# Self attention of a PixArt block: y is turned one step later, and VectorE takes its work of a step in another order

## The chip, the cores and the metric

One core of one Trainium2 chip runs the whole program. The metric is the device time of one execution, in microseconds, as the median of several runs; lower is better. The profile is of one execution, taken by the hardware profiler, and its times count from the start of its span.

## The reference

A transformer block on x of 16 batches, 224 tokens and 512 channels, with a context of 750 tokens: self attention with 16 heads of 32 channels, modulated by a condition, then cross attention on the context, then an MLP. The part that this change touches is the self attention and the query projection of the cross attention:

```python
x_norm = modulate(_ln(x), shift_a, scale_a)
qkv = x_norm @ W_qkv + b_qkv
attn_w = softmax(einsum('bhqd,bhkd->bhqk', q, k) * scale)
attn_out = einsum('bhqk,bhkd->bhqd', attn_w, v) @ W_proj + b_proj
x = x + gate_a[:, None] * attn_out
q_c = _ln(x) @ W_qc + b_qc
```

## The kernel before

The program has three phases one after another: self attention, cross attention, MLP. Each projection is made of three products of a split into a high and a low part (helper `product`, lines 71 to 73), so it takes three matmuls for each piece of 128 input channels.

The self phase is a pipeline over batches that is written out by hand. One body per batch has 16 steps, one per head; 19 bodies run, the last three to drain what lags. In step h of body b each engine runs its own list for that step, and every engine is a queue in order:

- TensorE (`pe`): the transposed scores of a head that lags by six (`score_t`, L487), the first projection of the step, the turning of row maxima at the end of a group of four heads (`turn_maxima`, L473), the scores of head h+1 (`score`, L455), the second projection of the step, if any, the value product and the sums of a group (`pv` L504 and `sums` L511, in steps 2, 6, 10, 14), and the turnings of x or y (`turn_x`, `turn_y`, both through `trans`, L418).
- VectorE (`dve`): the copy of turned maxima (`copy_maxima`, L714), normalisation of a group (`normalize`, L719 reciprocal and L722 product, in steps 0, 4, 8, 12), the row maxima of head h+1 (`row_max`, L701), their split into two parts in every fourth step (`split_maxima`, L707, L709), the evictions of the step's projections (`evict`: `lows` L656 for k, q and c, `add_bias` L666 for p, nothing for v), then the modulation of turned x (`modulate`, L649), the low part of turned y (`low_y`, L675), and others.
- ScalarE: the exponentials (L907), the high part of an eviction (L893, ahead of VectorE's `lows`), the high part of turned y (L918), the high part of o (L913), the layer norms (L875).
- GpSimd: the sum of two halves of the exponentials (L1017), the residual (L1025, L1027), the low part of x (L1009).

`FILL` is the table that says which projections and turnings are in which step: `("k", c, part)` is half `part` of the projection k of bank c. Letters k, q, v work for the next batch, p for the previous one, c (the query of the cross attention) for that two or three back. `tx` turns x of the batch two ahead (steps 12 and 13), `ty` turns y of the batch two back. An eviction follows the second half of a projection (`part == 1`). There is one bank of PSUM for each c, so the next projection on a bank waits until the last one is evicted (`bank_free`). `turn_x` for c == 1 waits for the modulation of c == 0 (`xT_v`), since both use the bank `tx_ps`; `turn_y` for c == 1 waits for `low_y` of c == 0 (`yT_l`) for the same reason, and for c == 0 it waits for the copy of the group's maxima (`m_row`), which use that bank too. Scores have two banks: `score` of a head waits for the row maxima of the head two before. `pv` of a group waits for `normalize` of the group before it (`o_done`).

Body 0 has no projections p and c, body 1 none of c, and body 1 has two products of the modulation (L561) in steps 13 and 14. From body 14 on no x is turned, and in body 15 there are no projections k, q, v.

Of the kernel before, what the change touches and what calls it, by code (L numbers as in the profile page):

```python
# [62 lines left out]
def wait(eng, sem, value):  # L63

    if not (isinstance(value, int) and value <= 0):
        eng.wait_ge(sem, value)
# [38 lines left out]
def self_phase(nc, x, cond_t, w_mod, b_mod, w_qkv, b_qkv_t, w_proj, b_proj, w_qc, b_qc_t, gates, x1, qc, mod_t,  # L105
# [3 lines left out]
    with ExitStack() as ctx:  # L109
# [109 lines left out]

        FILL = [[("c", 1, 1), ("k", 0, 0)], [("k", 0, 1)], [("k", 1, 0)], [("k", 1, 1), ("ty", 0, 0)],
# [3 lines left out]
        BANKS = [f for step in FILL for f in step if f[0][0] != "t" and f[2] == 0]  # L226

        def of(f):

            return -3 if f == ("c", 1, 1) else {"k": 1, "q": 1, "v": 1, "p": -1, "c": -2, "tx": 2, "ty": -2}[f[0]]  # L230

        def exists(b, f):
            return 0 <= b.c + of(f) < B and b.c >= -1

        def fills(b, h, kinds):
            return [(*f, b.plus(of(f))) for f in FILL[h] if f[0] in kinds and exists(b, f)]

# [23 lines left out]
        def far(b):  # L261
            return b.c < B - 2
# [11 lines left out]
        def late_group(b, h, att, prv):  # L274

            if h % HPG != (LAG + HPG) % HPG:
                return []
            g = (h - LAG - HPG) // HPG
            if g >= 0:
                return [(b, g)] if att else []  # L280
            return [(b.plus(-1), g + KC)] if prv else []
# [344 lines left out]
        def _(dve):  # L626
# [26 lines left out]
            def lows(b, c, high, low, bias, first_chunk, dst):  # L653
                dve.wait_ge(high, b.n(2, c + 1))
                for m in range(2):
                    last = dve.scalar_tensor_tensor(out=dst[1][:, 2 * c + m], in0=pj_ps[c][:, m * N:(m + 1) * N],  # L656
                                                    scalar=bias[:, first_chunk + m:first_chunk + m + 1],
                                                    in1=dst[0][:, 2 * c + m].bitcast(F32), op0=ALU.add, op1=ALU.subtract)
                last.then_inc(low, 1)

            def add_bias(b, t):
                dve.wait_ge(proj_ps, b.n(2, t + 1))
                wait(dve, x1_out, b.n(32, 0))
                if b.c == 0:
                    dve.wait_ge(bproj_in, 16)
                dve.tensor_tensor(y[:, t], pj_ps[t][0:QN, :], bproj[:], ALU.add).then_inc(proj_done, 1)  # L666
# [16 lines left out]
            def stats_context(t):  # L683
                dve.wait_ge(c_loaded[t], 16)
                dve.bn_stats(st_c[:, t], c_in[:, t]).then_inc(stats_c, 1)
# [12 lines left out]
            def row_max(b, h):  # L698
                g, j = h // HPG, h % HPG
                dve.wait_ge(scored, b.n(NH, h + 1))  # L700
                dve.tensor_reduce(nmax[:, g % 2, :, j], sc_ps[h % 2][0:QN, 0:QT * N].rearrange("p (t k) -> p t k", t=QT), AX_X, ALU.max,  # L701
                                  negate=True).then_inc(maxed, 1)

            def split_maxima(b, g):
                dve.wait_ge(maxed, b.n(NH, HPG * (g + 1)))
                wait(dve, m_ps, b.n(KC, g - 1))
                dve.tensor_copy(nsplit[:, g % 2, :, 0], nmax[:, g % 2]).then_inc(m_h, 1)  # L707
                dve.wait_ge(m_h, b.n(KC, g + 1))
                dve.tensor_tensor(nsplit[:, g % 2, :, 1], nmax[:, g % 2], nsplit[:, g % 2, :, 0].bitcast(F32), ALU.subtract).then_inc(m_l, 1)  # L709

            def copy_maxima(b, g):
                dve.wait_ge(m_ps, b.n(KC, g + 1))
                wait(dve, m_in, b.n(16 * KC, 16 * g))
                dve.tensor_copy(mrow[:], tx_ps[0:2 * HPG, 0:N]).then_inc(m_row, 1)  # L714

            def normalize(b, g):
                dve.wait_ge(sum_ps, b.n(KC, g + 1))
                wait(dve, o_done, b.n(KC, g))
                dve.reciprocal(rb[:], or_ps[:, R0:R0 + N]).then_inc(inverted, 1)  # L719
                dve.wait_ge(pv_done, b.n(KC, g + 1))  # L720
                dve.wait_ge(inverted, b.n(KC, g + 1))
                dve.tensor_tensor(ou[:], or_ps[:, 0:N], rb[:], ALU.mult).then_inc(o_done, 1)  # L722

            def evict(kind, c, part, o):
                if kind == "k" and part == 1:
                    lows(o, c, k_h, k_l, bqkv, KC + 2 * c, nat)
                if kind == "q" and part == 1:
                    lows(o, c, q_h, q_l, bqs, 2 * c, natq)
                if kind == "c" and part == 1:
                    lows(o, c, c_h, c_l, bqcs, 2 * c, natq)  # L730
                if kind == "p" and part == 1:
                    add_bias(o, c)

            def body(b, att, nxt, prv, old):
                z, y2, far_b = b.plus(-1), b.plus(-2), b.plus(2)
                for h in range(NH):
                    if h % HPG == HPG - 1 and att:
                        copy_maxima(b, h // HPG)
                    for o, g in late_group(b, h - 2, att, prv):
                        normalize(o, g)  # L740
                    if h < NH - 1 and att:
                        row_max(b, h + 1)
                    if h == NH - 1 and nxt:
                        row_max(b.plus(1), 0)
                    if h % HPG == HPG - 2 and att:
                        split_maxima(b, h // HPG)
                    for f in fills(b, h, "kqcp"):
                        evict(*f)
                    for _, c, _, o in fills(b, h, ("tx",)):
                        modulate(o, c)  # L750
                    for _, c, _, o in fills(b, h, ("ty",)):
                        low_y(o, c)
                    if h == 14 and att:
                        low_o(b, 0)
                    if h in LOW_O and prv:
                        low_o(z, LOW_O[h])
                    if far(b) and h == 6:
                        stats(far_b, x_in, x_loaded, lambda t: far_b.n(16, 0), st1, mv1, stats1, mvs1)
                    if far(b) and h == 8:
                        neg_mean(far_b, mv1, rs1, nm1, rstd1, nmr1)  # L760
                    if prv and h == 15:
                        stats(z, y, summed, lambda t: z.n(2, t + 1), st2, mv2, stats2, mvs2)
                    if old and h == 0:
                        neg_mean(y2, mv2, rs2, nm2, rstd2, nmr2)
                    if b.c == 0 and 2 <= h < 2 + KC:
                        low_w(3 * KC + h - 2)
                    if b.c == 1 and h == 0:
                        gate_rows(3)
                    if b.c == 1 and h in (13, 14):
                        mlp_row(h - 9)  # L770
                    if b.c == 1 and h == 15:
                        keep_modulation()
                    if b.c == 2 and 5 <= h < 5 + KC:
                        low_w(4 * KC + h - 5)
                    if b.c == B - 1 and 5 <= h < 5 + KC:
                        low_wkv(h - 5)
                    if b.c == B - 1 and 9 <= h < 9 + ST:
                        stats_context(h - 9)
                    if b.c == B and h == 0:
                        aggregate_context()  # L780
                    if b.c == B and h == 2:
                        neg_mean_context()
# [302 lines left out]
def cross_phase(nc, ctx_in_dram, b_kvc_t, qc, o_dram, wkv, c_in, cT, nat, pieces, ident, neg_half, eps):  # L1085
# [4 lines left out]
    with ExitStack() as ctx:  # L1090
# [50 lines left out]

        FILL = [[("k", 0, 0)], [("k", 0, 1)], [("k", 1, 0)], [("k", 1, 1)], [], [("k", 2, 0)], [("k", 2, 1)], [], [("v", 0)], [("k", 3, 0)], [("k", 3, 1), ("c", 0)], [("v", 1), ("c", 1)], [("v", 2), ("c", 2)], [("v", 3), ("c", 3)], [("v", 4), ("c", 4)], [("v", 5), ("c", 5)]]
        ORDER = [f for step in FILL for f in step if f[0] != "c"]

# [23 lines left out]
        def fill_at(b, h, kinds):  # L1168

            return [(f, b) for f in FILL[h] if f[0] in kinds and exists(b, f[0])]  # L1170

# [29 lines left out]

        STEP = {f[1]: h for h, step in enumerate(FILL) for f in step if f[0] == "c"}

# [998 lines left out]
```

## Time and profile before

| what | value |
|---|---|
| median of 3 runs | 2776.03 us (2774.58 to 2776.41) |
| span of the profiled execution | 2771.8 us |
| TensorE busy | 2667.6 us (96%) |
| VectorE busy | 1743.5 us (63%) |
| GpSimd busy | 1296.9 us (47%) |
| ScalarE busy | 1118.3 us (40%) |
| self phase | from 0 to about 770 us |
| one body of it in the steady part | 43.4 us |

A busy TensorE is not one at its peak: its matmuls are pipelined and their ends are modelled, so the distance from one start to the next says more than the busy time. An idle time in brackets at the end of a row, with the releaser, counts from the modelled end of the instruction before; the real loss is found from starts.

### The profile page before, as it was taken

To read this page: it belongs to the slowest core of one execution; us is meant where nothing else is said; L and a number is where in the kernel's file an instruction comes from. 1 tells how busy PE (TensorE), PEld (TensorE's weight loads), DVE (VectorE), ACT (ScalarE), POOL (GpSimd) and SP (SyncE) were. 2 spreads that over 40 slices of the span, in tenths; PEclk is the share of its full clock that TensorE was granted. 3 is DMA by queue.
4 is the path that set the end of the run, shared out by engine and by line. 5 is a ranking of instruction groups with operands and counts; after the bars stand their busy time and mean duration, and the time that the engine had idled before them with its cause. 6 is when DMAs were issued, how large, how long until landed. Compare 5 with 4: busy or idle time off the path is not lost. (4 is left out here: it accounts for less than half of the span.)

```text
span 2771.8 us, 50094 instructions
## 1 busy us (share of the span) xinstructions
PE 2667.6 (96%) x18676; PEld 2153.0 (78%) x18676; DVE 1743.5 (63%) x3285; ACT 1118.3 (40%) x2187; POOL 1296.9 (47%) x1447
## 2 busy tenths in 40 slices
PE   8999999999789999999999999999889999999997
PEld 6788888887677778777877877777568888888886
DVE  6777777777636777777777766776754444444431
ACT  4344444444434555555545555554532212112110
POOL 2344545444414676776676676666811220220211
PEclk9999999999899999999999999999789999999999
DMA  8454453545252443444344434433431111111110
GB/s 225 125 129 122 124 138 106 130 121 144 91 136 77 110 110 105 106 109 115 105 108 117 108 103 117 109 80 96 126 110 39 36 52 35 42 46 35 42 42 23
DMA packets 169359, 269.86 MB, mean 97 GB/s; under 512 B 28928, under 2 KB 83200, under 8 KB 169104
## 3 DMA queue, kind: packets, MB, share of 16 engines
q1 hardware_dynamic: 166048, 259.33, 34.5%
q0 software_dynamic: 3072, 7.34, 0.8%
q8 instruction: 150, 2.46, 0.4%
q14 instruction: 89, 0.73, 0.1%
HBM read 111.11 MB, written 36.77 MB: 53 GB/s over the span
## 5 line engine op out<-in xcount | busy, mean ns | idle before, releaser
L1490 DVE TENSOR_REDUCE cross_nmax<-cross_sc_ps 112x1 f32<-112x750 f32 x512 | 459.6, 928 | 162.7 <-PE cross_sc_ps L1365 162.6
L1608 ACT ACTIVATE cross_prT<-cross_tr_ps 125x448 f32<-125x448 f32 x768 | 389.9, 544 | 153.5 <-PE cross_tr_ps L1384 146.2
L1655 POOL TENSOR_TENSOR cross_part<-cross_prT 125x448 f32<-125x448 f32 x252 | 290.9, 1154 | 149.4 <-PE cross_or_ps L1404 83.4
L1017 POOL TENSOR_TENSOR self_psum<-self_prT 112x224 f32<-112x224 f32 x256 | 173.3, 677 | 349.4 <-ACT self_prT L907 337.0
L1384 PE MATMUL cross_tr_ps<-cross_qst,cross_kst 98*125 98x224 f32 x1536 | 314.4, 291 | 8.5 <-ACT cross_prT L1608 3.9
L1384 PEld LDWEIGHTS cross_tr_ps<-cross_qst,cross_kst 98*125 98x125 f32 x1536 | 244.6, 190 | 92.8 <-ACT cross_prT L1608 39.2
L1657 POOL TENSOR_TENSOR cross_part<-cross_part,cross_prT 125x448 f32<-125x448 f32 x252 | 291.9, 1158 | 19.8
L2052 ACT ACTIVATE mlp_hv<-mlp_h_ps,mlp_b 128x512 f32<-128x512 f32 x112 | 77.1, 689 | 519.8 <-PE mlp_h_ps L73 505.7
L1365 PE MATMUL cross_sc_ps<-cross_kst,cross_qst 96*112 96x500 f32 (+1 forms) x1024 | 274.2, 350 | 5.5 <-DVE cross_nmax L1490 2.3
L1969 DVE CAST mlp_hT_h<-mlp_hv 128x512 fp32r<-128x512 f32 x112 | 53.5, 477 | 319.1 <-ACT mlp_hv L2052 319.1
L907 ACT ACTIVATE self_prT<-self_st_ps 112x448 f32<-112x448 f32 x256 | 139.1, 544 | 210.6 <-PE self_st_ps L487 210.5
L701 DVE TENSOR_REDUCE self_nmax<-self_sc_ps 112x2 f32<-112x448 f32 x256 | 157.7, 617 | 79.5 <-PE self_sc_ps L455 78.5
L1659 POOL TENSOR_TENSOR cross_psum<-cross_part 125x224 f32<-125x224 f32 x252 | 170.2, 675 | 19.8
L71 PE MATMUL mlp_a_ps<-mlp_w_l,mlp_hT_h 128*128 128x512 f32 x448 | 178.3, 398 | 0.0
L72 PE MATMUL mlp_h_ps<-mlp_xT_h,mlp_w_l 128*128 128x512 f32 x448 | 177.5, 396 | 0.0
L72 PE MATMUL mlp_a_ps<-mlp_w_h,mlp_hT_l 128*128 128x512 f32 x448 | 176.9, 395 | 0.0
L73 PE MATMUL mlp_h_ps<-mlp_xT_h,mlp_w_h 128*128 128x512 f32 x448 | 176.7, 395 | 0.0
L73 PE MATMUL mlp_a_ps<-mlp_w_h,mlp_hT_h 128*128 128x512 f32 x448 | 176.6, 394 | 0.0
L71 PE MATMUL mlp_h_ps<-mlp_xT_l,mlp_w_h 128*128 128x512 f32 x448 | 176.6, 394 | 0.0
L71 PE MATMUL cross_pj_ps<-cross_cT_l,cross_wkv_h 128*128 128x374 f32 (+1 forms) x492 | 168.3, 342 | 4.3 <-DVE cross_nat_l L1484 4.3
L73 PE MATMUL cross_pj_ps<-cross_cT_h,cross_wkv_h 128*128 128x374 f32 (+1 forms) x492 | 165.5, 336 | 0.0
L1397 PE MATMUL cross_or_ps<-cross_prT,cross_vt 125*32 125x224 f32 x3072 | 164.8, 364 | 0.6 <-ACT cross_prT L1608 0.6
(247 smaller groups left out, 6644.9 us busy)
## 6 DMA issues: line engine op xcount, KB each, us to landing
cross_kst<-cross_nat_h SPq DMA_DIRECT2D x512, 93.8 KB, 2.2
cross_c_in<-in_context SPq DMA_DIRECT2D x96, 250.0 KB
cross_kst<-cross_nat_l SPq DMA_DIRECT2D x256, 93.8 KB, 2.2
cross_qst<-qc SPq DMA_DIRECT2D x192, 112.0 KB, 2.4
self_kst<-self_nat_h SPq DMA_DIRECT2D x128, 112.0 KB, 2.3
self_qst<-self_natq_h SPq DMA_DIRECT2D x128, 112.0 KB, 3.1
self_x_in<-in_x SPq DMA_DIRECT2D x16, 448.0 KB, 3.8
self_kst<-self_nat_l SPq DMA_DIRECT2D x64, 112.0 KB, 2.3
```

The source lines that it names most:

```text
L71: pe.matmul(out, lhs[0], rhs[1], start=first, stop=False)
L72: pe.matmul(out, lhs[1], rhs[0], start=False, stop=False)
L73: return pe.matmul(out, lhs[0], rhs[0], start=False, stop=last)
L1017: pool.tensor_tensor(psum[:, j], prT[:, j, 0], prT[:, j, 1], ALU.add).then_inc(p_summed, 1)
L1365: last = pe.matmul(sc_ps[t][0:QN, SC0 + c0:SC0 + c0 + cn], qst[0:TERMS * HD, g, j, t * QN:(t + 1) * QN], kst[0:TERMS * HD, g, j, c0:c0 + c ...
L1384: last = pe.matmul(bank(step, c)[0:SN, m * N:(m + 1) * N], kst[:, g, j, kt * SN:(kt + 1) * SN], qst[:, g, j, :], start=True, stop=True)
L1397: last = pe.matmul(or_ps[HD * j:HD * j + HD, 0:N], vt[:, b.par, kt, h * HD:h * HD + HD], prT[:, slot(h), kt], start=kt == 0, stop=kt == ST ...
L1490: dve.tensor_reduce(nmax[:, g % 2, t, j:j + 1], sc_ps[t][0:QN, SC0:SC0 + S], AX_X, ALU.max, negate=True).then_inc(maxed, 1)
L1608: act.activation(prT[:, slot(h), 2 * c:2 * c + 2], bank((h + LAG) % NH, c)[0:SN, 0:2 * N].rearrange("p (k t) -> p k t", k=2), ACT.Exp).the ...
L1655: pool.tensor_tensor(part[:], prT[:, j, 0:2], prT[:, j, 2:4], ALU.add).then_inc(pre_summed, 1)
L1657: pool.tensor_tensor(part[:], part[:], prT[:, j, 4:6], ALU.add).then_inc(pre_summed, 1)
L1659: pool.tensor_tensor(psum[:, j], part[:, 0], part[:, 1], ALU.add).then_inc(p_summed, 1)
```

## The change

Two things. In the table `FILL` the two turnings of y move from steps 3 and 4 to steps 4 and 5; TensorE's `turn_y`, ScalarE's high part and VectorE's low part follow, since all three read the table. In VectorE's list of a step, the eviction that belongs to the step's first entry now stands right behind the copy of maxima, then come the row maxima and their split, then the evictions of the other entries, and then normalisation, which stood ahead of the row maxima. The letter v is added to the kinds only so that "first entry" counts it; its eviction does nothing on VectorE.

```diff
-        FILL = [[("c", 1, 1), ("k", 0, 0)], [("k", 0, 1)], [("k", 1, 0)], [("k", 1, 1), ("ty", 0, 0)],
-                [("q", 0, 0), ("ty", 1, 0)], [("q", 0, 1), ("q", 1, 0)], [("q", 1, 1)], [("v", 0, 0)],
+        FILL = [[("c", 1, 1), ("k", 0, 0)], [("k", 0, 1)], [("k", 1, 0)], [("k", 1, 1)],
+                [("q", 0, 0), ("ty", 0, 0)], [("q", 0, 1), ("q", 1, 0), ("ty", 1, 0)], [("q", 1, 1)], [("v", 0, 0)],
                 [("v", 0, 1), ("v", 1, 0)], [("v", 1, 1)], [("p", 0, 0)], [("p", 0, 1), ("p", 1, 0)],
                 [("p", 1, 1), ("tx", 0, 0)], [("c", 0, 0), ("tx", 1, 0)], [("c", 0, 1)], [("c", 1, 0)]]
...
                 for h in range(NH):
                     if h % HPG == HPG - 1 and att:
                         copy_maxima(b, h // HPG)
-                    for o, g in late_group(b, h - 2, att, prv):
-                        normalize(o, g)
+                    for f in fills(b, h, "kqcpv")[0:1]:
+                        evict(*f)
                     if h < NH - 1 and att:
                         row_max(b, h + 1)
                     if h == NH - 1 and nxt:
                         row_max(b.plus(1), 0)
                     if h % HPG == HPG - 2 and att:
                         split_maxima(b, h // HPG)
-                    for f in fills(b, h, "kqcp"):
+                    for f in fills(b, h, "kqcpv")[1:]:
                         evict(*f)
+                    for o, g in late_group(b, h - 2, att, prv):
+                        normalize(o, g)
```

## Rows read from the trace of the kernel before

**Rows 1.** The page's first part: busy time, share of the span, instructions.
```profile
PE 2667.6 (96%) x18676; PEld 2153.0 (78%) x18676; DVE 1743.5 (63%) x3285; ACT 1118.3 (40%) x2187; POOL 1296.9 (47%) x1447
```
**Rows 2.** Who TensorE waited for, 130 to 660: total us, times, longest us.
```profile
PE self_tx_ps L418 <- DVE self_mrow L714: 3.4, 13, 0.3
PE self_pj_ps L71 <- DVE self_natq_l L656: 2.7, 12, 0.2
```
**Rows 3.** Timeline, TensorE, steps 2 and 3 of body 6: start, length, [idle before].
```profile
300.87 0.38 PE L487 MATMUL self_st_ps<-self_qst,self_kst 98*112 98x224 f32 x2
301.46 0.37 PE L71 MATMUL self_pj_ps<-self_xT_l,self_wqkv_h 128*128 128x224 f32 x1 [0.22 <-DVE self_natq_l L656]
...
306.24 0.44 PE L455 MATMUL self_sc_ps<-self_kst,self_qst 96*112 96x224 f32 x2
306.94 0.60 PE L418 MATMUL self_tx_ps<-shared_ident,self_x_res 112*128 112x112 f32 x4 [0.26 <-DVE self_mrow L714]
```
**Rows 4.** Timeline, TensorE, where it waits for nothing: score, score_t, projection.
```profile
317.56 0.44 PE L455 MATMUL self_sc_ps<-self_kst,self_qst 96*112 96x224 f32 x2
317.84 0.37 PE L487 MATMUL self_st_ps<-self_qst,self_kst 98*112 98x224 f32 x2
318.05 0.39 PE L71 MATMUL self_pj_ps<-self_wqkv_l,self_xT_h 128*112 128x512 f32 x1
```
**Rows 5.** Timeline, VectorE, step 12 of body 6, whole.
```profile
329.54 1.53 DVE L719 RECIPROCAL self_rb<-self_or_ps 128x224 f32<-128x224 f32 x1
331.18 0.39 DVE L722 TENSOR_TENSOR self_ou<-self_or_ps,self_rb 128x224 f32<-128x224 f32 x1
331.51 0.63 DVE L701 TENSOR_REDUCE self_nmax<-self_sc_ps 112x2 f32<-112x448 f32 x1
332.05 0.68 DVE L666 TENSOR_TENSOR self_y<-self_pj_ps,self_bproj 112x512 f32<-112x512 f32 x1
332.65 0.92 DVE L649 TENSOR_SCALAR self_xv<-self_tx_ps,shared_mod_t 128x224 f32<-128x224 f32 x2
```
**Rows 6.** Timeline, TensorE, the end of step 12 and of step 13 of body 6.
```profile
330.87 0.39 PE L73 MATMUL self_pj_ps<-self_wproj_h,self_oT_h 128*112 128x512 f32 x1
...
333.63 0.60 PE L418 MATMUL self_tx_ps<-shared_ident,self_x_in 112*128 112x112 f32 x4
```
**Rows 7.** Timeline, TensorE, the second projection of step 0 of body 7.
```profile
341.00 0.28 PE L71 MATMUL self_pj_ps<-self_xT_l,self_wqkv_h 128*128 128x224 f32 x1
...
342.50 0.27 PE L487 MATMUL self_st_ps<-self_qst,self_kst 98*112 98x224 f32 x1
```
**Rows 8.** Windows: us, busy (instructions) of PE, PEld, DVE, ACT, POOL; PEclk, DMA, GB/s.
```profile
68.20:71.00 2.80, 0.00 (x0) 0.00 (x1) 2.70 (x6) 0.36 (x2) 1.11 (x2) 1.00 0.82 182
72.20:75.40 3.20, 3.20 (x29) 1.60 (x28) 2.68 (x5) 1.00 (x2) 1.81 (x2) 0.50 0.00 0
686.60:689.80 3.20, 1.45 (x12) 1.10 (x10) 3.05 (x8) 1.39 (x4) 1.67 (x4) 1.00 0.01 2
690.00:710.30 20.30, 18.10 (x100) 12.40 (x100) 17.25 (x31) 11.46 (x20) 7.52 (x9) 0.50 0.35 115
809.40:816.10 6.70, 5.17 (x28) 4.28 (x28) 1.95 (x3) 2.36 (x5) 0.00 (x0) 1.00 0.56 132
```
**Rows 9.** Timeline, TensorE, like matmuls at 1.2 GHz, then at 2.4 GHz.
```profile
758.37 0.41 PE L73 MATMUL self_pj_ps<-self_yT_h,self_wqc_h 128*128 128x224 f32 x1
758.58 0.41 PE L71 MATMUL self_pj_ps<-self_yT_l,self_wqc_h 128*128 128x224 f32 x1
...
762.38 0.27 PE L71 MATMUL self_pj_ps<-self_yT_l,self_wqc_h 128*128 128x224 f32 x1
762.49 0.28 PE L72 MATMUL self_pj_ps<-self_yT_h,self_wqc_l 128*128 128x224 f32 x1
```
**Rows 10.** Timeline, the split of maxima on VectorE and GpSimd's residual, step 14.
```profile
336.69 0.73 DVE L707 CAST self_nsplit<-self_nmax 112x8 fp32r<-112x8 f32 x1
...
336.11 1.28 POOL L1027 TENSOR_TENSOR self_y<-self_y,self_x_res 112x512 f32<-112x512 f32 x1
```

## The prediction

> **What bounds the kernel now.** The page's first part says that TensorE is busy for 96% of the span and VectorE for 63% [rows 1], so the program is as long as TensorE's work plus what TensorE loses in waits. The change touches the self phase alone, about 770 us, and there its steady part: bodies 2 to 14, 43.4 us each. Next I read who TensorE waited for in that part. The answer has two lines [rows 2]: 13 waits of the first turning of y (L418) for the copied maxima, and 12 of the projection in step 2 (L71) for an eviction of c. The reader should see that these are exactly the two things that the diff loosens, and that they are small. Then I read the timelines of TensorE and VectorE of body 6, since every body repeats them within some hundredths. The lost time is to be taken from starts, not from the idle time in brackets, because the ends are modelled.
>
> **Removed: the wait in step 2.** The eviction of c on bank 1 stands behind normalisation and a reduction in step 0 and ends late. The projection starts 0.59 us after the `score_t` ahead of it [rows 3]; where nothing is waited for, that distance is 0.21 us [rows 4]. So 0.38 us is lost, 12 times [rows 2]: 4.6 us. With the eviction first in step 0 it ends about 2 us earlier, and the wait is gone for good.
>
> **Removed: the wait of the first turning of y.** It starts 0.70 us after the score [rows 3]; a score behind a turning of maxima otherwise gives way after 0.28 us [rows 4]. So 0.42 us, 13 times: 5.5 us. One step later its maxima have been copied for some 2 us.
>
> **Moved: the second turning of y, to the end of step 5.** It waits for VectorE's low part of the first, which now stands behind normalisation in step 4. VectorE needs there 0.54 for a reduction, 1.97 for a normalisation (both below) and for the low part about what a reduction over as many columns takes, 0.63 [rows 5]: 3.1 us from the score of step 4. TensorE has meanwhile a turning, `score_t`, two projections of twelve matmuls at 0.11 us [rows 9] and a score, about 3.4 us. It fits with 0.1 to 0.3 us to spare, so I cost it at nothing; the other bound is 0.3 us in 13 bodies, 4 us. ScalarE's high part of o comes behind the high part of y in step 5, under a microsecond later, and nobody waits for it before step 10. On SyncE's queue the load of x for the residual follows the maxima of step 7, so it doesn't see the move.
>
> **Added: normalisation behind an eviction, in step 12.** This is the costly one. In step 12 VectorE now does, in a row [rows 5]: reciprocal 329.54, product 331.18, row maxima 331.51, `add_bias` 332.05, modulation of the first half of x 332.65 to 333.57. At 333.63 TensorE turns the second half of x [rows 6], which waits for just that modulation: the chain already touches TensorE. The reader should see that normalisation runs while TensorE is still at the projection p of that step, whose last matmul starts at 330.87 and ends at 331.26 [rows 6]: it costs nothing there. In the new order VectorE comes first to `add_bias`, which needs that projection. Normalisation waits behind it in the queue though everything that it needs is there. The new chain, in the clock of body 6: `add_bias` 331.30; its distance to the next instruction 0.60 (332.65 - 332.05), so row maxima at 331.90; 0.54 (332.05 - 331.51), so normalisation at 332.44; 1.64 to the product and 0.33 to the next (331.18 - 329.54, 331.51 - 331.18), so modulation at 334.41; 0.92 long, so 335.33; and 0.06 to TensorE's start as now (333.63 - 333.57): 335.39 instead of 333.63. I take 1.75 us per body; the bounds, from overlaps of up to a tenth at each end, are 1.6 and 1.9.
>
> It doesn't happen in every body. From body 14 on no x is turned. Body 0 has no projection p, so nothing stands ahead of normalisation. In body 1 TensorE has eight matmuls of the modulation between the two turnings, long enough to hide it. Bodies 2 to 13 are left: 12 times 1.75, 21.0 us.
>
> **Given back by the longer body.** The second projection of step 0 takes 1.50 us from its first start to the next instruction [rows 7], against 12 times 0.11, 1.32 [rows 9]: it waits for GpSimd's low part of x inside. GpSimd's work doesn't get later by the stall, so this 0.18 us goes, 12 times: 2.2 us.
>
> **The other steps with normalisation.** In steps 0, 4 and 8 it ends 1 to 1.6 us later against TensorE. Its readers on TensorE (`pv` two steps later) stand about 3 us behind, and ScalarE, which waits longer for it in step 8, is ahead of TensorE by more than a step. Cost nothing, bound 0.1 us per body.
>
> **Body 15 and the tail.** Body 15 has no second projection in step 0, so TensorE waits 2.1 us for row maxima there and is then granted half the clock for 20 us (0.50 from 690.0 to 710.3) [rows 8]. The new order gives the maxima 1 us earlier and normalisation 1.5 us later, for which `pv` waits: about +0.3. If the clock stayed up, VectorE, busy for 17.25 of these 20.30 us [rows 8], leaves at most 3 us to gain. So 0, bounds -3 and +2. The bodies behind it drain and hold nothing of the change that is longer than some tenths.
>
> **The sum without the clock.** -4.6 - 5.5 - 2.2 + 21.0 = +8.7 us. The profiled execution spans 2771.8 us, 4.2 us under the median; the sum stands for both: 2776.0 + 8.7 = 2784.7.
>
> **The clock.** The new idle time is 1.75 us more than the wait of some 0.2 us that is there now, so about 1.9 us in one piece, in each of 12 bodies. What idle time does to TensorE's clock here: after nothing ran from 68.20 to 71.00 the granted clock was 0.50 (1.2 GHz) from 72.20 to 75.40; after the 2.1 us idle in body 15 it was 0.50 for 20 us; around an idle time of 1.53 us (6.70 less 5.17, from 809.40 to 816.10) it stayed at 1.00 (2.4 GHz) [rows 8]. The new idle time lies between 1.5 and 2.1 us. I take it that half of the 12 bodies, six, see a drop. The short one here covers the whole of 72.20 to 75.40, so I take 3.4 us for one at the lower clock; there like matmuls start every 0.21 us instead of every 0.11 [rows 9]: 3.4 times (1 - 0.11/0.21) = 1.6 us. Six are 9.7 us; none and twelve are the bounds, 0 and 19. The long drop of body 15 isn't taken: TensorE was short of work there, while behind the turning of x a projection of twelve matmuls and a value product are ready.
>
> **A rule that bears on the split of maxima.** In steps 6 and 14 it now comes behind an eviction, about 0.4 us ahead of the turning that needs it. The row of step 14 shows a cast that took 0.73 us and ended at 337.42, as GpSimd's residual did at 337.39 [rows 10]. The Trainium skill, page SBUF — State Buffer, section "Who interferes with whom", says that VectorE, in a two-port mode or with two inputs in SBUF, and GpSimd take one shared pair of ports for a whole instruction, and that the later one blocks. By that rule the split, moved against GpSimd's work, could be held again; the trace agrees that it can. In rows: a GpSimd sum or product of 0.7 to 1.3 us hides 0.4 us of margin and would cost 0.3 to 0.6 us in some bodies. It is a rival below.
>
> **The rivals.** (a) The stall is there, but the clock holds: 2785. For it: 1.53 us didn't drop it. Against: 2.1 us did. (b) Not slower: step 12 costs TensorE nothing, because VectorE reaches modulation in time. It decides at 12.3 us of gain over 12 bodies, so at 1.0 us of new stall per body: `add_bias` through modulation would have to take 3.3 us rather than 4.1. Without a stall: 2776.0 - 12.3 = 2764. Against it stands the sum of five rows in one queue; for it, only that a projection's end is modelled. (c) More waits: the split held by GpSimd and the second turning of y late by its bound: 0.5 us in 12 bodies on top of the forecast, 2801. (d) The clock stays low for 20 us after each drop as in body 15: a drop then costs 20 times 0.48, 9.6 us, six of them 58: 2843.
>
> **How the numbers follow.** Forecast, stall and about six short drops: 0.50, 2784.7 + 9.7 = 2794, itself 2787 to 2806. (a) 0.27, 2781 to 2788. (b) 0.07. (c) 0.11, 2797 to 2810. (d) 0.05. The range from 2780 to 2806 leaves out (b), (d) and part of (c). A measurement of this kernel can tell about 0.2%, 5.5 us, from no change: faster is under 2770.5, slower over 2781.5. Faster 0.05 of (b); same 0.02 of (b) and 0.07 of the low end of (a), where fewer bodies stall; slower the rest, 0.86.
>
> **What would show it.** Right: TensorE waits for modulation (L649) about 1.9 us in 12 bodies, after which VectorE's order is `add_bias`, row maxima, reciprocal, product, modulation; both lines of [rows 2] are gone; the distance between bodies is about 44.2 us where the clock holds. Wrong: the second turning of x starts within 0.4 us of its score; or a wait at L473 for the split (L709), or of the second turning of y for L675. The granted clock behind each stall tells the forecast from (a) and (d). The figure most open is the number of drops.

## The result and the profile after

The changed kernel takes 2792.1 us (four runs, 2790.4 to 2795.3) against 2776.2 us before; the ratio is 1.0055, 95% interval 1.0043 to 1.0068. Forecast was 2794 in a range from 2780 to 2806, slower with 0.86. The profiled execution spans 2793.2 us, 21.4 us more than that of before; it is the slowest of the four runs.

Who TensorE waited for in bodies 2 to 14 of the changed kernel, from 130 to 680: total us, times, longest us.

```profile
PE self_tx_ps L418 <- DVE self_xv L649: 21.5, 12, 2.1
PE self_or_ps L504 <- ACT self_prT L909: 0.4, 1, 0.4
```

Both lines of [rows 2] are gone. In their place stands one that before had not: 12 waits of the second turning of x for the modulation, 21.5 us: 1.76 us in eleven of the bodies and 2.1 us in body 8. The timeline of VectorE in step 12 of one body, and of TensorE at the end of steps 12 and 13 of it:

```profile
339.67 0.69 DVE L666 TENSOR_TENSOR self_y<-self_pj_ps,self_bproj 112x512 f32<-112x512 f32 x1 [1.69 <-PE self_pj_ps L73]
340.28 0.62 DVE L701 TENSOR_REDUCE self_nmax<-self_sc_ps 112x2 f32<-112x448 f32 x1
340.81 1.55 DVE L719 RECIPROCAL self_rb<-self_or_ps 128x224 f32<-128x224 f32 x1
342.46 0.39 DVE L722 TENSOR_TENSOR self_ou<-self_or_ps,self_rb 128x224 f32<-128x224 f32 x1
342.77 0.92 DVE L649 TENSOR_SCALAR self_xv<-self_tx_ps,shared_mod_t 128x224 f32<-128x224 f32 x2
```

```profile
339.24 0.39 PE L73 MATMUL self_pj_ps<-self_wproj_h,self_oT_h 128*112 128x512 f32 x1
...
341.62 0.37 PE L455 MATMUL self_sc_ps<-self_kst,self_qst 96*112 96x224 f32 x2
343.75 0.61 PE L418 MATMUL self_tx_ps<-shared_ident,self_x_in 112*128 112x112 f32 x4 [1.76 <-DVE self_xv L649]
```

These are the instructions of [rows 5] and [rows 6] in their new order. VectorE is idle for 1.69 us ahead of `add_bias`, the time in which it had normalised before. From the end of the projection (339.63) to TensorE's start (343.75) the chain takes 4.12 us; the forecast had 4.13.

The granted clock, one row for each of bodies 2 to 13, from the first score of one to that of the next. The columns are those of [rows 8]; the number ahead of the last two is TensorE's clock.

```profile
124.87:171.45 46.58, 43.79 (x375) 36.66 (x373) 35.07 (x75) 22.02 (x45) 22.03 (x27) 0.96 0.46 118
171.45:215.45 44.00, 42.24 (x379) 36.25 (x377) 32.53 (x72) 20.41 (x42) 20.60 (x27) 1.00 0.46 122
215.45:261.07 45.62, 43.86 (x379) 37.87 (x377) 32.53 (x72) 20.49 (x42) 20.89 (x27) 0.96 0.45 118
261.07:305.07 44.00, 42.24 (x379) 36.26 (x377) 32.53 (x72) 20.41 (x42) 20.92 (x27) 1.00 0.46 122
...
393.07:440.43 47.36, 45.25 (x379) 38.43 (x377) 32.52 (x72) 20.48 (x42) 20.89 (x27) 0.93 0.44 114
440.43:486.04 45.61, 43.85 (x379) 37.80 (x377) 32.52 (x72) 20.48 (x42) 20.59 (x27) 0.96 0.45 117
...
618.05:663.66 45.61, 43.85 (x380) 37.86 (x377) 32.53 (x72) 20.48 (x42) 20.91 (x27) 0.96 0.46 118
sum 538.79, PE 516.31 PEld 442.39 DVE 392.88 ACT 246.82 POOL 251.33; mean PE 43.03 PEld 36.87 DVE 32.74 ACT 20.57 POOL 20.94
```

A body is 44.00 us long where the clock held (before: 43.38) and 45.61 us where it dropped once; body 2 is 1 us longer for other reasons, with and without a drop. Five of the twelve have a drop; that at 0.93, 47.36 us long, has one twice as long, and is the body with the wait of 2.1 us. The five rows left out at "..." are like the one of 44.00 us. VectorE is busy for 32.5 us in either kind of body: the 1.6 us are TensorE's alone.

Where the 21.4 us of the profiled execution lie, from the starts of bodies: 2.5 us up to body 2; 18.6 us in bodies 2 to 13 (538.79 against 520.20); -0.5 us in body 14; 3.2 us in the drain; and -2.2 us in the cross and MLP phases, where nothing was changed. Over all traces of this case these two phases take 1996.5 to 2000.2 us, so 3 us of a single execution can come from there alone; the comparisons of bodies below are free of it.

### The profile page after: what moved, and what is told of

Its sections match the earlier page's. It is cut to its first block and busy times, and to the rows that moved or that the text cites. A ratio compares the mean times of both kernels' runs of the same rounds, so it can differ in the third digit from the quotient of the medians.

```text
span 2793.2 us, 50094 instructions
## 1 busy us (share of the span) xinstructions
PE 2666.8 (95%) x18676; PEld 2158.8 (77%) x18676; DVE 1738.7 (62%) x3285; ACT 1115.7 (40%) x2187; POOL 1304.0 (47%) x1447
## 5 line engine op out<-in xcount | busy, mean ns | idle before, releaser
L1019 POOL TENSOR_TENSOR self_psum<-self_prT 112x224 f32<-112x224 f32 x256 | 184.9, 722 | 342.3 <-ACT self_prT L909 333.5
L72 PE MATMUL cross_pj_ps<-cross_cT_h,cross_wkv_l 128*128 128x374 f32 (+1 forms) x492 | 165.5, 336 | 0.0
```

The source lines that it names most:

```text
L72: pe.matmul(out, lhs[1], rhs[0], start=False, stop=False)
L1019: pool.tensor_tensor(psum[:, j], prT[:, j, 0], prT[:, j, 1], ALU.add).then_inc(p_summed, 1)
```

## The experiments

Two theories stand against each other at first. T: the loss is made in step 12 alone, where normalisation waits behind `add_bias`, and all else is gain. R: it is spread over the four normalisations of a body, and the late turning of y adds to it. A third question is what part of the loss is the clock (theory C).

**The table alone.** The edit is that of the change in `FILL`; VectorE's list is that of before.

> The kernel before with the table of the change alone (y turned in steps 4 and 5, VectorE's order as before). Two theories. T: the whole loss of the change is made in step 12, where normalisation stands behind add_bias, and the move of y is a gain. R: the loss is spread over the four normalisations of a body, a quarter each, and the late turning of y adds to it. T expects the wait for copied maxima at L418 to be gone in 13 bodies, bodies 0.4 to 0.5 us shorter (43.38 to about 42.9 us), so 13 times 0.48, -6 us: 2770, 2768 to 2773. R expects no gain or a loss: 2776 or more.

It takes 2768.9 us, ratio 0.9973 (0.9961 to 0.9984). What TensorE waited for in bodies 2 to 14:

```profile
PE self_pj_ps L71 <- DVE self_natq_l L656: 2.4, 12, 0.2
```

The wait for copied maxima is gone, that of step 2 is left, and a body is 42.89 us long, 0.49 us shorter. The late turning of y is a gain.

**VectorE's order alone.** Here `FILL` is that of before.

> VectorE's new order alone, y turned in steps 3 and 4 as before. T: all that the change lost and 6 us more, since the gain of the table is missing: 2792 + 6 = 2798 (2794 to 2803), with the stall of 1.76 us ahead of the second turning of x in bodies 2 to 13, and the wait for copied maxima back. R: less than the whole change, about 2786 to 2790, since the late turning of y is undone.

2797.4 us, ratio 1.0073 (1.0061 to 1.0086). Its waits in bodies 2 to 14:

```profile
PE self_tx_ps L418 <- DVE self_xv L649: 21.4, 12, 2.1
PE self_tx_ps L418 <- DVE self_mrow L714: 3.4, 13, 0.3
```

The new order carries the whole loss, and the table took some of it back: 5 us by the medians, 44.48 us for a body against 44.00.

**Step 12 in the old order, all else changed.**

```diff
+                    if h == 12:
+                        for o, g in late_group(b, h - 2, att, prv):
+                            normalize(o, g)
                     for f in fills(b, h, "kqcpv")[0:1]:
                         evict(*f)
...
-                    for o, g in late_group(b, h - 2, att, prv):
-                        normalize(o, g)
+                    if h != 12:
+                        for o, g in late_group(b, h - 2, att, prv):
+                            normalize(o, g)
```

> The changed kernel, with normalisation back at the head of step 12 and nowhere else. T: no stall ahead of the second turning of x and no drop of the granted clock in bodies 2 to 13; what is left are the gains, 6 us of the table and 5.6 us of step 2, less some 5 us that body 1 and the drain lose by the new order: 2770, 2766 to 2773. R: a quarter of the loss goes, so about 2785 to 2788.

2773.1 us, ratio 0.9989 (0.9980 to 0.9998): 19 us less than the changed kernel, by one normalisation of four put back. That is at the upper edge of what T expected, and R is out. But it is slower than the table alone, and the reason is a wait that was not there before (waits in bodies 2 to 14, then VectorE, GpSimd and TensorE in steps 14 and 15 of one body):

```profile
PE self_tx_ps L473 <- DVE self_nsplit L709: 5.9, 12, 0.5
```

```profile
338.11 0.62 DVE L701 TENSOR_REDUCE self_nmax<-self_sc_ps 112x2 f32<-112x448 f32 x1
338.76 0.17 DVE L707 CAST self_nsplit<-self_nmax 112x8 fp32r<-112x8 f32 x1
338.97 1.14 DVE L709 TENSOR_TENSOR self_nsplit<-self_nmax,self_nsplit 112x8 fp32r<-112x8 f32 x1
...
338.94 1.14 POOL L1015 TENSOR_TENSOR self_xT_l<-self_xv,self_xT_h 128x448 fp32r<-128x448 f32 x1
...
340.16 0.35 PE L473 MATMUL self_tx_ps<-shared_ident,self_nsplit 112*8 112x112 f32 x2 [0.51 <-DVE self_nsplit L709]
```

The second instruction of the split, 0.17 us where nothing holds it, starts 0.03 us behind GpSimd's low part of x and ends with it, at 340.11 and 340.08. That is the rival (c) of the prediction, as the Trainium skill has it (page SBUF — State Buffer, section "Who interferes with whom"): two inputs in SBUF on VectorE contend with a GpSimd instruction that reads SBUF, and the later one is held for the whole of it. The rows agree. In the changed kernel the split of step 14 isn't held in any of bodies 2 to 13: the longer wait ahead of it puts it between two low parts of x on GpSimd (346.55 to 347.70, then from 349.56), and both its instructions take 0.17 us.

```profile
348.22 0.17 DVE L707 CAST self_nsplit<-self_nmax 112x8 fp32r<-112x8 f32 x1
348.43 0.17 DVE L709 TENSOR_TENSOR self_nsplit<-self_nmax,self_nsplit 112x8 fp32r<-112x8 f32 x1
```

**The same, with the split of step 14 ahead of the eviction.**

```diff
-                    for f in fills(b, h, "kqcpv")[0:1]:
+                    for f in fills(b, h, "kqcpv")[0:0 if h == 14 else 1]:
                         evict(*f)
...
-                    for f in fills(b, h, "kqcpv")[1:]:
+                    for f in fills(b, h, "kqcpv")[0 if h == 14 else 1:]:
                         evict(*f)
```

> The kernel with normalisation first in step 12 (2773), with the eviction of step 14 behind the split of maxima again. In that kernel the second instruction of the split takes 1.13 instead of 0.17 us in step 14, to the end of GpSimd's low part of x, and TensorE waits 0.5 us for it in 12 bodies. If this wait is the missing part of the gain, its bodies are 0.5 to 0.6 us shorter, 42.3 us, and the time is 2773 - 6.5 = 2767 (2765 to 2769), 12 waits at L473 gone. If the missing part is lost in body 1, the drain or by late normalisation, nothing changes: 2772 to 2774.

2767.7 us, ratio 0.9966 (0.9954 to 0.9979). The 12 waits at L473 are gone and a body is 42.41 us long instead of 42.87. The split is still held in one of its instructions, by 0.6 us, but early enough:

```profile
335.19 0.77 DVE L707 CAST self_nsplit<-self_nmax 112x8 fp32r<-112x8 f32 x1
335.99 0.17 DVE L709 TENSOR_TENSOR self_nsplit<-self_nmax,self_nsplit 112x8 fp32r<-112x8 f32 x1
```

**Step 12 alone in the new order, all else as before.**

```diff
-                    for o, g in late_group(b, h - 2, att, prv):
-                        normalize(o, g)
+                    if h != 12:
+                        for o, g in late_group(b, h - 2, att, prv):
+                            normalize(o, g)
+                    if h == 12:
+                        for f in fills(b, h, "kqcp"):
+                            evict(*f)
...
-                    for f in fills(b, h, "kqcp"):
-                        evict(*f)
+                    if h != 12:
+                        for f in fills(b, h, "kqcp"):
+                            evict(*f)
+                    if h == 12:
+                        for o, g in late_group(b, h - 2, att, prv):
+                            normalize(o, g)
```

> The kernel before, with the new order in step 12 alone (evictions, row maxima, then normalisation). T: 12 stalls of 1.75 us more, 21 us, less 2 us given back in step 0, and four to six drops of the granted clock at 1.6 us: 2776 + 19 + 8 = 2803, 2797 to 2808, so slower than the whole change. R: a quarter of it, about 2783.

2807.1 us, ratio 1.0108 (1.0094 to 1.0122), 15 us slower than the whole change, as T expects. A body is 45.13 us long where the clock held, 1.75 us more than before, and six of the twelve have a drop. The 2 us that T took off as given back in step 0 are not in the time: the projection there waits no longer for GpSimd, but the one of step 2 then waits more for the eviction of c, 0.4 us instead of 0.2.

```profile
PE self_pj_ps L71 <- DVE self_natq_l L656: 4.7, 12, 0.4
```

**The idle time filled.** 14 matmuls whose result nobody reads are put ahead of the second turning of x; the computation is unchanged.

```diff
+                    if h == 13 and far(b) and b.c > 1:
+                        pe.wait_ge(proj_done, b.n(2, 0))
+                        for _ in range(14):
+                            pe.matmul(pj_ps[1][:, 0:N], wqkv[0][:, 0, 0:P], wqkv[0][:, 1, 0:N], start=True, stop=True)
```

> The changed kernel, with 14 matmuls of 128x224 whose result nobody reads put where TensorE sits idle in step 13 of bodies 2 to 13, ahead of the second turning of x (14 times 0.11 = 1.6 us of the 1.76 us stall). The chain on VectorE, and so the stall's end, stays. Theory C: about 10 us of the 16 us lost are drops of the granted clock that the idle time brings. It expects no drop in bodies 2 to 13, bodies of 44.0 us throughout, and 2783 (2780 to 2786). Rival: the drops have another cause or cost nothing, 2792 as the changed kernel, or more.

2787.2 us, ratio 1.0041 (1.0028 to 1.0053). TensorE in step 13 of one body, then windows over bodies 2 to 13:

```profile
339.64 1.73 PE L596 MATMUL self_pj_ps<-self_wqkv_h 128*128 128x224 f32 x14
341.56 0.60 PE L418 MATMUL self_tx_ps<-shared_ident,self_x_in 112*128 112x112 f32 x4 [0.19 <-DVE self_xv L653]
```

```profile
125.00:341.00 216.00, 214.21 (x1895) 183.99 (x1891) 161.15 (x355) 100.46 (x206) 101.03 (x127) 1.00 0.48 123
341.00:668.00 327.00, 325.10 (x2922) 281.58 (x2921) 241.90 (x540) 152.90 (x316) 157.55 (x195) 1.00 0.46 119
```

More work on TensorE makes the kernel faster: the turning waits as long as before, but no body has a drop, and they are 44.00 us long (body 2: 45.01, body 8: 44.35). From the first score of body 2 to that of body 14 it takes 529.3 us, against 538.8 in the changed kernel and 520.2 before. So of the 18.6 us there, 9.5 are the clock, 1.6 for each of the five drops and as much again for the long one, and 9.1 the waits less what the change gained. The median fell by 5 us only, less than the 9 expected, and lies 1 us over the range of theory C; the profiled execution of the changed kernel was the slowest of its four, and the one of its repetition below has fewer drops.

**Seven of them, half the idle time left.** The edit is the same with `range(7)`.

> The changed kernel with 7 instead of 14 unread matmuls in the stall, so that 1.0 us of idle time is left in one piece. The short stall of 1.22 us saw no drop, so theory C expects none here: bodies of 44.0 us and 2787 as with 14. If any idle time of this place can drop the clock, some drops come back: 2789 to 2792.

2789.7 us, ratio 1.0044 (1.0031 to 1.0057). In its trace TensorE is idle for 1.0 us in a piece ahead of the turning and the clock doesn't drop there. The median lies in the range of the second expectation, but its trace bears out the first: from the first score of body 2 to that of body 14 it takes 529.3 us, as with 14 matmuls. The profiled execution is 3.5 us longer than that with 14, and 3.2 of them lie in the cross and MLP phases. Whether some of its other runs had drops isn't known.

**The changed kernel once more.**

> The changed kernel, beside the two others on one chip, since its runs spread over 5 us (2790.4 to 2795.3). If that spread is the number of drops, 0 to 6 of them at 1.6 us, its median is again near 2792 (2790 to 2794) and its spread wider than that of the kernel with 14 unread matmuls (2786.7 to 2789.7).

2794.7 us, ratio 1.0063 (1.0050 to 1.0076), with four drops in bodies 2 to 13 of its trace (bodies 2, 3, 8 and 13; in the first trace they were 2, 4, 8, 9 and 13). Its runs spread over 3.6 us and those with 14 unread matmuls over 3.0 us, so the spread alone proves nothing. Both measurements of the changed kernel lie 5 and 7.5 us over the one with the idle time filled: by an estimate from that, three to five drops at 1.6 us in a usual run.

**A shorter stall.** The row maxima of step 12 come behind the modulation.

```diff
-                    if h < NH - 1 and att:
+                    if h < NH - 1 and h != 12 and att:
                         row_max(b, h + 1)
...
                     for _, c, _, o in fills(b, h, ("tx",)):
                         modulate(o, c)
+                    if h == 12 and att:
+                        row_max(b, h + 1)
```

> The changed kernel, with the row maxima of step 12 behind the modulation, so that the chain from add_bias to modulation is one reduction shorter: a stall of about 1.22 instead of 1.76 us. By the sum the 12 bodies are 0.54 us shorter, 6.5 us. Theory C (a shorter idle time drops the clock less often) expects at most one or two drops in bodies 2 to 13: 2792 - 6.5 - 6 to 8 = 2778 (2775 to 2781). Rival, each stall has its chance of a drop whatever its length: five drops still, 2785.

2780.6 us, ratio 1.0015 (1.0007 to 1.0024), 11.5 us less than the changed kernel though the chain is only 12 times 0.54 us, 6.5 us, shorter. The rest is the clock, which drops in none of bodies 2 to 13. From the first score of body 2 to that of body 14 it takes 522.7 us, 6.6 less than with the idle time filled and 16.1 less than the changed kernel. Its waits in bodies 2 to 14:

```profile
PE self_tx_ps L418 <- DVE self_xv L649: 14.9, 12, 1.4
```

That is 1.22 us in eleven bodies and 1.39 in body 8. The rival, for which each stall has its chance of a drop, expected 2785 and is out.

**A longer stall.** One reduction more, unread, ahead of the row maxima of step 12.

```diff
+        waste = sb("waste", [QN, QT])
...
+                    if h == 12 and 1 < b.c < B - 2:
+                        dve.wait_ge(scored, b.n(NH, h + 2))
+                        dve.tensor_reduce(waste[:], sc_ps[1][0:QN, 0:QT * N].rearrange("p (t k) -> p t k", t=QT), AX_X, ALU.max, negate=True)
                     if h < NH - 1 and att:
                         row_max(b, h + 1)
```

> The changed kernel with one more reduction, whose result nobody reads, ahead of the row maxima of step 12 in bodies 2 to 13: the stall grows from 1.76 to about 2.3 us and bodies to 44.54 us, 6.5 us in all. Theory C (the length of the idle time decides on the drop) expects 9 to 12 drops: 2792 + 6.5 + 8 = 2806 (2801 to 2811). Theory P (what decides is where in time the stalls fall, since VectorE's order alone, with the same stall 44.48 us apart, had one drop and step 12 alone, 45.13 us apart, six) expects a number like that of bodies 44.48 us apart, 0 to 3: 2792 + 6.5 - 4 = 2794 (2791 to 2799).

2806.3 us, ratio 1.0112 (1.0097 to 1.0127): the time of theory C. Its trace doesn't bear C out, though: it has five drops where C expected 9 to 12. The profiled execution is 8.9 us longer than that of the changed kernel, and only 4.5 of them lie in bodies 2 to 13 (543.25 against 538.79); the rest lies ahead of body 2 and behind body 14, so that the time agrees with C is in part luck. Waits in bodies 2 to 13, then the clock over bodies 3 to 9 and over the four behind:

```profile
PE self_tx_ps L419 <- DVE self_xv L650: 27.5, 12, 2.3
```

```profile
173.00:526.00 353.00, 334.68 (x2970) 287.45 (x2970) 262.10 (x579) 161.09 (x332) 164.44 (x206) 1.00 0.47 121
526.00:668.00 142.00, 135.13 (x1156) 115.28 (x1158) 100.05 (x221) 62.56 (x130) 64.61 (x81) 0.95 0.44 115
```

Idle times of 2.3 us dropped the clock in body 2, then left it up seven times in a row (each of these bodies is 44.53 us long) and dropped it in the last four. And VectorE's order alone, with the stall of the changed kernel, had one drop in the twelve bodies, in body 2 (first row); bodies 3 to 13 are 44.48 us long, body 8 with its longer wait 44.83:

```profile
167.60:170.90 3.30, 3.30 (x29) 2.33 (x31) 1.25 (x4) 1.24 (x3) 2.33 (x3) 0.50 0.23 70
172.00:680.00 508.00, 485.18 (x4313) 416.16 (x4312) 370.85 (x824) 235.94 (x484) 237.36 (x296) 1.00 0.46 119
```

So length and count don't go together above 1.7 us: 1.0 and 1.2 us gave none of twelve; 1.76 us (and 2.1 in body 8) gave one, four, five and six in four kernels or runs; 2.3 us gave five. When an idle time falls decides as well as how long it is, since equal ones had different outcomes, in one kernel from run to run and in one trace from body to body. In what way is left open: no run here moved the idle time and kept its length.

**A version for both.** Normalisation waits behind the eviction in step 0 alone, and only in bodies with an eviction of c to bring forward and another projection behind it; step 12 keeps normalisation first and takes eviction and modulation ahead of the row maxima.

```diff
-                    for f in fills(b, h, "kqcpv")[0:1]:
-                        evict(*f)
+                    if not (h == 0 and 2 < b.c < B - 1):
+                        for o, g in late_group(b, h - 2, att, prv):
+                            normalize(o, g)
+                    if (h == 0 and 2 < b.c < B - 1) or h == 12:
+                        for f in fills(b, h, "kqcp"):
+                            evict(*f)
+                    if h == 12:
+                        for _, c, _, o in fills(b, h, ("tx",)):
+                            modulate(o, c)
                     if h < NH - 1 and att:
                         row_max(b, h + 1)
+                    if h == 0 and 2 < b.c < B - 1:
+                        for o, g in late_group(b, h - 2, att, prv):
+                            normalize(o, g)
...
-                    for f in fills(b, h, "kqcpv")[1:]:
-                        evict(*f)
-                    for o, g in late_group(b, h - 2, att, prv):
-                        normalize(o, g)
-                    for _, c, _, o in fills(b, h, ("tx",)):
-                        modulate(o, c)
+                    if not ((h == 0 and 2 < b.c < B - 1) or h == 12):
+                        for f in fills(b, h, "kqcp"):
+                            evict(*f)
+                    if h != 12:
+                        for _, c, _, o in fills(b, h, ("tx",)):
+                            modulate(o, c)
```

> A version for both: the table of the change; in step 0 of bodies 3 to 14 evictions, row maxima, normalisation; in every other step VectorE's order of before, but in step 12 normalisation, then eviction and modulation, then row maxima. By theory T: the table alone measured 2769; 12 waits of step 2 go, 5.6 us, and the wait of some 0.25 us ahead of the second turning of x, 3 us: 2760 (2757 to 2764). If normalisation late in step 0 costs as the rival R has it, 2768 or more.

2762.2 us, ratio 0.9950 (0.9937 to 0.9964), 14 us faster than before and 30 us faster than the change. TensorE waits for VectorE in none of bodies 2 to 14; a body is 42.41 us long. Late normalisation in step 0 costs nothing.

One wait is left that the list of waits doesn't name: in step 0 the second projection waits in its middle for GpSimd's low part of x. From its first start to the next instruction it takes 1.72 us, against 1.34 where nothing is waited for (GpSimd, then two TensorE rows in step 0 of one body):

```profile
337.96 1.15 POOL L1021 TENSOR_TENSOR self_xT_l<-self_xv,self_xT_h 128x448 fp32r<-128x448 f32 x1
...
338.77 0.27 PE L73 MATMUL self_pj_ps<-self_xT_h,self_wqkv_h 128*128 128x224 f32 x1
339.17 0.37 PE L71 MATMUL self_pj_ps<-self_xT_l,self_wqkv_h 128*128 128x224 f32 x1
```

The two matmuls start 0.40 us apart instead of 0.11. In the kernel with the split of step 14 first, whose bodies are 42.41 us long too, the projection takes 1.56 us and the second turning of x still waits, 0.34 us behind its score instead of 0.21. So what this version gains in step 13 it loses again in step 0, and the 3 us that were expected of it are not in the time. GpSimd works there without a gap of 0.1 us from 331.45 to 339.11, so a further gain would have to begin with its list; that wasn't tried.

## Why the prediction was right, step by step

**The wait of step 2** (0.38 us, 12 times) and **that of y** (0.42 us, 13 times) are gone. The second was worth 0.49 us by the table alone, and the first about 0.48. The working took the distance to the waiting instruction and left out that the first instruction behind a wait also gives way later: the waiting projection took 1.44 us from its start at 301.46 to the next score at 302.90, where one that waits for nothing takes 1.34 (309.74 to 311.08, both in the trace of before). That is why a body is 44.00 us long where the working had about 44.2.

**The second turning of y** had a margin of 0.1 to 0.3 us in the working. It starts at 320.62, 1.34 us after the projection ahead of it, so it waits for nothing, and the low part before it ends at 320.45.

**The chain of step 12** was 4.12 us against 4.13, in the twelve bodies named. Body 0 waited 2.8 us as before. This term, 21 us, carries the forecast, and step 12 put back alone takes it away.

**Given back.** The low part of x no longer holds the projection of step 0. With the clock up, the waits cost 9.1 us in bodies 2 to 13. The working, for those bodies, had 21.0 - 2.2 less 12 times 0.42 less 11 times 0.38, 9.6.

**The clock** was forecast as six drops of 1.6 us, 9.7 us. The profiled execution has 9.5 us of it. In a usual run it is 5 to 7.5 us, so this term was some 3 us too large, and the way it was reached, by the length of the idle time against lengths of 1.5 and 2.1 us, is only half the truth, as the long stall shows. That the count came near six is luck: the same stall in VectorE's order alone gave one.

**Body 1 and the drain** were taken at 0 and cost some 1.3 and 3 us; the second is outside the bound of 2 us that the working gave. In body 1 the rows of the gates stand behind normalisation in step 0, and the projection that waits for them (L800) loses 1.4 us; the forecast had not gone through body 1's own list:

```profile
PE self_pj_ps L71 <- DVE self_wm_gates L800: 1.4, 1, 1.4
```

In the drain TensorE waits for late normalisation itself, 3.7 us in two waits, where before there was one of 1.2 us:

```profile
PE self_or_ps L504 <- DVE self_ou L722: 3.7, 2, 2.1
```

These misses and the clock's cancel, so 2792 against 2794 says less than the terms do.

**The rivals.** (a), a clock that holds, is what the kernel with the idle time filled shows: 2787, where the sum said 2785. (b) is out. (c) doesn't cost anything in the changed kernel and 0.5 us per body as soon as the stall is taken away. (d), a long drop behind each stall, didn't come: one of the five was twice the length, 6.8 us, and none longer.

## What to carry to other kernels

An instruction that waits in an engine's queue holds all behind it: before an order is turned to match another engine's, ask of each step whether the one that moves forward has its input yet, and what was done in that time. A change that is a gain in some steps and a loss in one is read step by step, and each step can then be had by itself. Where TensorE must wait for one or two microseconds again and again, the clock can add a good part to the waits: here 5 to 9.5 us to the 21 us of the waits. Work that nobody reads, in the gap, then shortens the kernel.

## What was not expected of the hardware

TensorE's granted clock fell from 2.4 to 1.2 GHz behind idle times of 1.76 us in some bodies and not in others that were alike to 0.01 us, and idle times of 2.3 us were passed over seven times in a row. A split of 8 columns that takes 0.17 us took 1.14 us beside a GpSimd instruction that had started 0.03 us before it. And 14 matmuls more in each of twelve bodies made the kernel 5 us faster.
